# Loading and normalising the residual in one block, four transfers instead of one

## What is computed

```
m = mean(x, axis=-1);  v = var(x, axis=-1)
xn = (x - m) / sqrt(v + 1e-5)                  # the layer norm, no gain, no shift
q  = xn @ Wq.T + bq                            # 16 heads of 16
k, v = ctx @ Wk.T + bk, ctx @ Wv.T + bv        # from the context, not from x
x  = x + softmax((q k + relative terms) / 4) (v + relative terms) @ Wo.T + bo
... mixture 0, attention 1, mixture 1
```

## Time and profile before

| | us |
|---|---|
| median of three runs | 2146.1 |
| the profiled execution | 2133.87 |
| its span, first to last instruction | 2132.1 |
| TensorE busy in the span | 1902.6 |
| mean granted TensorE clock | 0.943 of full |

### The profile page before, as it was taken

The page is one execution under the profiler, slowest core; times in us unless marked ns, Lnnn a source line. Parts: engine busy times, 40 slices in busy tenths (PEclk is TensorE's granted clock), DMA queues, the critical chain, the costliest instruction groups (busy, mean ns, idle before and its releaser), DMA issues. The chain is left out here.

```text
span 2132.1 us, 40119 instructions
## 1 busy us (share of the span) xinstructions
PE 1902.6 (89%) x13656; PEld 1647.9 (77%) x13657; DVE 1329.4 (62%) x2964; ACT 1018.8 (48%) x1747; POOL 620.4 (29%) x555
## 2 busy tenths in 40 slices
PE   4788956999669999999999999999999983999994
PEld 3477956999558887887888888888888763899994
DVE  5174054667667777887787778877787875122223
ACT  2544413555246555555555565545555641444441
POOL 2300002333244423442344324422443101122220
PEclk9899967999779999999999999999999995899997
DMA  5502163111242123212322133113311218211114
GB/s 201 178 24 87 64 240 102 48 47 49 77 117 53 38 51 72 53 43 47 70 53 46 44 71 69 43 32 71 71 41 31 63 47 295 75 35 36 37 34 131
DMA packets 93663, 159.24 MB, mean 75 GB/s; under 512 B 22385, under 2 KB 54831, under 8 KB 91707
## 3 DMA queue, kind: packets, MB, share of 16 engines
q1 hardware_dynamic: 82875, 134.32, 22.4%
q0 software_dynamic: 8320, 20.65, 3.3%
q10 hardware_dynamic: 2304, 2.10, 0.3%
HBM read 71.57 MB, written 32.41 MB: 49 GB/s over the span
## 5 line engine op out<-in xcount | busy, mean ns | idle before, releaser
L1833 ACT ACTIVATE a_prob<-a_slot,a_npeak 128x848 f32<-128x848 f32 x256 | 248.4, 970 | 204.4 <-DVE a_npeak L1894 204.1
L1699 PE MATMUL a_slot<-a_KHL,a_QHL 128*128 128x424 f32 (+1 forms) x1536 | 299.5, 344 | 12.8 <-DVE a_probT L1915 10.9
L1892 DVE TENSOR_REDUCE a_part_peak<-a_slot 128x2 f32<-128x848 f32 x256 | 265.4, 1037 | 39.2 <-PE a_slot L1699 38.9
L1724 PE MATMUL a_po<-a_probT,a_V 128*64 128x256 f32 (+1 forms) x2304 | 276.8, 385 | 0.0
L1846 ACT ACTIVATE a_probT<-a_slot 128x640 f32<-128x640 f32 x256 | 180.6, 706 | 200.1 <-PE a_slot L1708 151.3
L1708 PE MATMUL a_slot<-ident,a_prob 128*128 128x128 f32 x2048 | 268.6, 275 | 0.0
L1699 PEld LDWEIGHTS a_slot<-a_KHL,a_QHL 128*128 128x128 f32 x1536 | 237.0, 190 | 39.2 <-issue 14.2
L1924 DVE CUSTOM_DVE_ANT_0 a_masked<-a_prob,a_maskr,a_latent_sum 128x253 f32<-128x253 f32 x256 | 183.5, 717 | 101.8 <-ACT a_prob L1835 86.9
L1708 PEld LDWEIGHTS a_slot<-ident,a_prob 128*128 128x128 f32 x2048 | 236.0, 142 | 8.7 <-issue 0.3
L1724 PEld LDWEIGHTS a_po<-a_probT,a_V 128*64 128x64 f32 (+1 forms) x2304 | 153.8, 136 | 83.2 <-issue 7.2
L1649 PEld LDWEIGHTS a_side<-a_W,a_latT 128*128 128x128 f32 x1536 | 193.8, 196 | 23.8 <-issue 10.8
(11 more groups left out here) (321 smaller groups left out, 3031.8 us busy)
## 6 DMA issues: line engine op xcount, KB each, us to landing
a_KHL<-a_KT SPq DMA_DIRECT2D x128, 256.0 KB, 4.4
a_QHL<-a_QT SPq DMA_DIRECT2D x128, 128.0 KB, 2.4
m_up<-_L_ffn_gate_up_proj_dram SPq DMA_DIRECT2D x8, 1024.0 KB, 9.4
m_up<-in_L_ffn_W_dram SPq DMA_DIRECT2D x8, 1024.0 KB, 9.1
m_down<-in_L_ffn_W_dram SPq DMA_DIRECT2D x8, 1024.0 KB, 12.5
a_prob_dram<-a0p_zeros SPq DMA_DIRECT2D x4, 1632.0 KB, 11.0
a_dist_dram<-a_dist SPq DMA_DIRECT2D x4, 1632.0 KB, 8.2
a_band_prob<-a_prob_dram SPq DMA_DIRECT2D x4, 1632.0 KB, 6.9
```

The source lines that it names most:

```text
L1699: ins = t_.matmul(out[:, i * BANK:i * BANK + hi - lo], q, KHL[:, pair.parity, h, part, lo:hi], start=part == 0, stop=part == 1)
L1724: ins = t_.matmul(po_t[h * D1:(h + 1) * D1, :], V[0:rows, pair.parity, j, h, :], probT[0:rows, gi % 2, j, h, :], start=j == PARTS[0][0], s ...
L1833: a_.activation(prob[:, u % 2, 0:2 * CUT].rearrange("p (n k) -> p n k", n=2), two_banks(slot[u % 2]), ACT.Exp, bias=bias, accum_out=latent ...
L1892: v.tensor_reduce(part[:, 0:2], two_banks(slot[u % 2]), AX.X, ALU.max).then_inc(part_peaked, 1)
```

## The change

`load_residual` and the weights' block are gone. `residual_norm` replaces `layer_norm`: one block in which SP issues four transfers of `x`, one for each group of four tiles and each with its own semaphore, then the identity, and then (through `load_rest`) the same twelve transfers of weights and constants in the same order. DVE waits for the transfer of group g ahead of that group's statistics, and PE waits for the identity ahead of its first transpose. The arithmetic, the sizes and the order on DVE, POOL, PE and ACT are as they were. The options of `layer_norm` that no call used are gone too.

```
+        @block.sync
+        def _(sp):
+            tiles = x.rearrange("b (t p) e -> p (b t) e", p=P)
+            for g in range(TILES // LN_GROUP):
+                cols = slice(g * LN_GROUP, (g + 1) * LN_GROUP)
+                sp.dma_start(xres[:, cols, :], tiles[:, cols, :]).then_inc(x_loaded[g], 16)
+            sp.dma_start(ident[:, :], ident_in).then_inc(ident_loaded, 16)
+            load_rest(sp)
+
         @block.vector
         def _(dve):
             def moments_of(g):
...
+                dve.wait_ge(x_loaded[g], 16)
                 for t in tiles:
-                    nc.vector.bn_stats(stats[:, t, :], src[:, t, :]).then_inc(stats_done, 1)
+                    nc.vector.bn_stats(stats[:, t, :], xres[:, t, :]).then_inc(stats_done, 1)
...
         @block.tensor
         def _(pe):
-            for t in range(TILES if dstT is not None else 0):
+            pe.wait_ge(ident_loaded, 16)
+            for t in range(TILES):
                 pe.wait_ge(dst_done, t + 1)
...
-def load_residual(nc, x, ident_in, xres, ident):
...
-            sp.dma_start(xres[:, :, :], x.rearrange("b (t p) e -> p (b t) e", p=P)).then_inc(x_loaded, 16)
-            sp.dma_start(ident[:, :], ident_in).then_inc(x_loaded, 16)
-            sp.wait_ge(x_loaded, 32)
...
-            with nc.Block() as block:
-                @block.sync
-                def _(sp):
-                    for n, dst in (("Wk", W["Wk"]), ("Wv", W["Wv"]), ("Wq", W["Wq"]), ("Wo", Wo)):
...
-            layer_norm(nc, "a0ln", xres, xn, ident, xnT)
+            def load_rest(sp):
+                for n, dst in (("Wk", W["Wk"]), ("Wv", W["Wv"]), ("Wq", W["Wq"]), ("Wo", Wo)):
...
+            residual_norm(nc, I["x"], I["ident"], xres, ident, xn, xnT, load_rest)
...
-        load_residual(nc, I["x"], I["ident"], xres, ident)
```

More of the change, by code:

```diff
@@ L83, in after, with residual_norm @@
         self.engine.wait_ge(self.sem, self.n)
-def layer_norm(nc, name, src, dst, ident, dstT=None, gain=None, shift=None, store=None):
+def residual_norm(nc, x, ident_in, xres, ident, xn, xnT, load_rest):
+    name = "a0ln"
     with phase(nc) as ctx:
@@ L98, in layer_norm @@
         turned = [ctx.enter_context(nc.psum_tensor(f"{name}_turned{i}", [P, EC, P], F32)) for i in range(4)]
+        x_loaded, ident_loaded = [sem(f"x_loaded{g}") for g in range(TILES // LN_GROUP)], sem("ident_loaded")
         stats_done, moments_done, variance_done = sem("stats_done"), sem("moments_done"), sem("variance_done")
@@ L123, in _ @@
                 for t in range(g * LN_GROUP, (g + 1) * LN_GROUP):
-                    nc.vector.tensor_scalar(dst[:, t, :], src[:, t, :], moments[:, t, 0:1], rstd[:, t:t + 1],
+                    nc.vector.tensor_scalar(xn[:, t, :], xres[:, t, :], moments[:, t, 0:1], rstd[:, t:t + 1],
                                             ALU.subtract, ALU.mult).then_inc(dst_done, 1)
@@ L142, in _ @@
                 for c in range(EC):
-                    ins = nc.tensor.transpose(turned[t % 4][:, c, :], dst[:, t, c * P:(c + 1) * P], ident[:, :])
+                    ins = nc.tensor.transpose(turned[t % 4][:, c, :], xn[:, t, c * P:(c + 1) * P], ident[:, :])
                 ins.then_inc(turned_done, 1)
@@ L147, in _ @@
         def _(act):
-            for t in range(TILES if dstT is not None else 0):
+            for t in range(TILES):
                 act.wait_ge(turned_done, t + 1)
[L150 to L157, removed]
-        @block.sync
-        def _(sp):
[L161 to L165, removed]
-def load_residual(nc, x, ident_in, xres, ident):
[L170 to L175, removed]
-            sp.dma_start(xres[:, :, :], x.rearrange("b (t p) e -> p (b t) e", p=P)).then_inc(x_loaded, 16)
-            sp.dma_start(ident[:, :], ident_in).then_inc(x_loaded, 16)
-            sp.wait_ge(x_loaded, 32)
+                nc.scalar.activation(xnT[:, :, t * P:(t + 1) * P], turned[t % 4][:, :, :], ACT.Copy).then_inc(copied, 1)
 class Context:
@@ L308, in layer0_attention @@
             loaded = sem2("loaded")
-            with nc.Block() as block:
-                @block.sync
-                def _(sp):
-                    for n, dst in (("Wk", W["Wk"]), ("Wv", W["Wv"]), ("Wq", W["Wq"]), ("Wo", Wo)):
[L313 to L321, removed]
-            layer_norm(nc, "a0ln", xres, xn, ident, xnT)
+            def load_rest(sp):
+                for n, dst in (("Wk", W["Wk"]), ("Wv", W["Wv"]), ("Wq", W["Wq"]), ("Wo", Wo)):
+                    sp.dma_start(dst[:, :, :], I["L0_xattn_" + n + "T"].rearrange("(c p) n -> p c n", p=P)).then_inc(loaded, 16)
+                sp.dma_start(ctxT[:, :, :], I["ctxT"].rearrange("(c p) n -> p c n", p=P)).then_inc(loaded, 16)
+                sp.dma_start(bq[:, :], I["L0_xattn_bq"]).then_inc(loaded, 16)
+                sp.dma_start(bk[:, :], I["L0_xattn_bk"]).then_inc(loaded, 16)
+                sp.dma_start(bv[:, :], I["L0_xattn_bv"].to_broadcast([CTX, E])).then_inc(loaded, 16)
+                sp.dma_start(rv0[:, :], I["rv_far"].to_broadcast([CTX, E])).then_inc(loaded, 16)
+                sp.dma_start(bo[:, :], I["L0_xattn_bo"].to_broadcast([P, E])).then_inc(loaded, 16)
+                sp.dma_start(mask[:, :], I["head_mask"]).then_inc(loaded, 16)
+                sp.dma_start(relk[:, :, :], I["rel_k"]).then_inc(loaded, 16)
+            residual_norm(nc, I["x"], I["ident"], xres, ident, xn, xnT, load_rest)
             pq = [c2.enter_context(nc.psum_tensor(f"a0_pq{i}", [P, BANK], F32)) for i in range(4)]
```

## The result

| | before | changed |
|---|---|---|
| first comparison, median (6 executions each) | 2135.77 us | 2119.19 us |
| ratio, 95% interval | | 0.9916, 0.9891 to 0.9941 |
| second comparison (26 and 5) | 2132.38 us | 2117.11 us, 0.9937 (0.9916 to 0.9958) |
| third comparison (16 and 9) | 2132.69 us | 2120.96 us, 0.9941 (0.9922 to 0.9959) |
| span of the profiled execution | 2132.1 us | 2117.2 us |

Forecast: 11.4 us faster, 2134.7 us. Measured: 11.7 to 16.6 us faster by the medians of three comparisons, 2119 us. The absolute number was 15.5 us off, most of it not the change's: the 2146.1 us of before was the median of three executions, and 78 further executions in the later comparisons have a median of 2133.0 us. Against that the changed kernel's 20 executions (median 2119.2 us) are 13.8 us faster, 2.4 us more than the shift.

A forecast was written before the change was run, and what follows sets the result against it. TensorE bounds the whole span, but the start is a chain of blocks separated by barriers. Norm start 16.07 to 4.7 gives -11.4 us, stalls, identity, weights and clearing 0: 2146.1 - 11.4 = 2134.7 us, range 2119 to 2146.

The forecast's parts named there:

- the shift: Whole kernel: everything behind the norm comes earlier by the norm's earlier start, 11.4 us, and the total falls by that.
- Bound and chain: Start of the kernel: 9 us of transfer, 6 us of issuing and 14 us of norm need not be in a row.
- the boundary behind the norm: End of the norm's block: the 1.10 us boundary stays, with 0 to +0.3 us for more semaphores to clear, taken as 0.
- Arrival of the first group: First block: group 0 of x is usable at 4.65, DVE starts at 4.7 instead of 16.07; bounds 4.0 and 9.3.
- No stalls, the identity hidden, the weights in time: Norm and next block: cost 0 each; later groups arrive with margins from 0.45 us, identity at 9.3, weights by 17.0.
- The splitting by itself costs nothing: First block: three further issues of x cost SP about 0.5 us each and lie under the transfer.
- rival A: First block: pieces of x land together or pay in a row; saving 6.8 or 7.7 us, time 2138 to 2141; 10%.
- The passing on through SP's clearing: Block 4: it ends with SP's clearing transfers, a chain tied to the block's start, so it moves by the full 11.4 us.
- Behind it nothing knows of absolute time but TensorE's clock: Everything behind block 4: stages keep their lengths, each 11.4 us earlier.
- The base: Whole kernel: the saving is taken off the median of 2146.1 us, not the profiled 2133.87 us, 12 us under it.
- Rival B: Behind the start: late clock returns, up to 2.1 us each, give the shift back; with twelve late +13.8 us, 2159.9 us; 5%.

The follow-up runs named there:

- four_apart: The kernel before with x in four transfers, all waited for in the first block: ratio to before 1.0008.
- zeros_early: The changed kernel with the memset of zeros and the four clearing transfers moved into the first block, behind the weights: ratio to before 0.9926.
- context_early: zeros_early with the nine small context loads also issued in the first block, ahead of the clearing: 2110.9 us, ratio to before 0.9898.
- late_inside: The changed kernel with SP first loading x whole and waiting for it inside the same block: ratio to before 0.9970.
- again1: The changed kernel run once more, unaltered: 2117.11 us, ratio to before 0.9937.
- again2: The changed kernel run a third time, unaltered: 2120.96 us, ratio to before 0.9941.
- filler_dve8: The changed kernel with eight already fulfilled waits added to DVE's program in the first block: 2124.1 us, ratio to before 0.9948.
- filler_dve: The changed kernel with four already fulfilled waits added to DVE's program ahead of its first statistics: 2119.6 us, ratio to before 0.9946.
- one_transfer: The changed kernel with x in one transfer, so DVE waits for all of it: ratio to before 0.9961.
- filler_pool: The changed kernel with eight already fulfilled waits added to POOL's program in the first block: ratio to before 0.9935.
- weights_apart: The changed kernel with the twelve weight transfers in a block of their own behind the norm: ratio to before 0.9951.
- extra_block: The changed kernel with a small block put ahead that loads only the identity and waits: ratio to before 0.9956.
- late_start: The changed kernel with the old first block ahead, x and the identity loaded, waited for, then loaded again: ratio to before 1.0000.
- filler_dve12: The changed kernel with twelve already fulfilled waits added to DVE's program in the first block: 2124.0 us, ratio to before 0.9946.

## Why the prediction was right and wrong

- **Bound and chain: right.** Three things in a row that need not be; the products moved by 11.46 us for a forecast of 11.4. That the two agree so closely is in part luck: DVE started 11.06 us earlier, and the boundary behind the norm, put at no change or up to 0.3 us more, took less (PE waits 1.22 us there instead of 1.56), which gives 0.34 us back. No run shows why it is shorter.
- **Arrival of the first group: right, 0.3 us small.** 5.01 for 4.7, within the bounds 4.0 to 9.3: from 2.5 to 3.0 us only 43 GB/s flowed with four transfers, against 223 with one.
- **No stalls, the identity hidden, the weights in time: right.** First transpose 9.77 (9.3), transfers through at 15 (17 at the latest), 5 us ahead of their use. SP's last weight issue ended at 10.64 (10.5).
- **The splitting by itself costs nothing: nearly.** 0.45 us in four_apart, where pieces that pay in a row had 7.1 us due, an estimate (rival A's 16.35 us less the 9.26 us of before); that part of rival A is out.
- **The passing on through SP's clearing: right.** zeros_early and context_early take that chain off, and the products move from 43.30 to 41.34 and 41.03 us.
- **The step that failed** is the sentence "Behind it nothing knows of absolute time but TensorE's clock", and with it the saving as a pure shift. The change also took instructions off DVE's program, a term that the sum didn't have: with 5592 instead of 5598 records three collisions with POOL's operations go the other way, 0.95 us each, 2.9 us. Time itself had no part in that: late_inside starts 7.5 us later and has the short passes. 11.4 + 2.9 = 14.3 us is inside the intervals of all three comparisons (one less the ratio, times the median of before: 12.6 to 23.3, 9.0 to 17.9 and 8.7 to 16.6 us), where 11.4 lies outside the first and inside the other two. So the 2.9 us are shown in the profiles, and the totals don't exclude a surplus of nothing or of more.
- **The base was mis-sized.** I took the saving off 2146.1, with the profiled 2133.87 in hand, and said only that they differ by 12 us. 13 us of the 15.5 us error are this median of three.
- **Rival B** (the clock gives it back) named the right source of scatter, with the wrong consequence: it moves single executions both ways (again1's and again2's profiles are 9.8 us apart, at a mean granted clock of 0.944 and 0.934), and no comparison shifted to slower. The clock's drop and return are in the records: in before PE idles from 50.34 to 54.76 us and the granted clock is 0.50 from 52.29 to 59.11; in the changed kernel PE idles from 37.09 to 43.30 and the clock is 0.50 from 39.17 to 49.41.

## What to carry to other kernels

A wait for a whole transfer, a block that only issues and a norm are three stages until they share a block; here the gain could be read off the start of the first consumer (11.06 us, and 11.46 us at the products), and it holds if the chain that ends the next block is tied to that block's start. When that chain is taken off as well, another engine ends the block: in context_early it was PE, and the slow pace of its first matmuls (2.39 us for eight, 1.29 us in the changed kernel), covered until then, came onto the path. When a stage has moved, compare the rest of the two profiles instruction by instruction before calling a surplus scatter: here the order of two engines, 0.03 us one way and 0.11 us the other, flipped with eight waits (filler_dve8) 1300 us ahead of it. And take a base time from more than three executions when the change is as small as their spread.

## What was not expected of the hardware

- The same DVE operation (line 1924 of before, 1905 of the changed kernel) took 1.52 us where POOL's `a_QT` operation (line 1613) had begun 0.03 us ahead of it, in before, and 0.48 us where it had begun 0.11 us ahead of POOL's, in the changed kernel; POOL's took 1.27 and 1.51 us.
- Eight waits on DVE that are already fulfilled (filler_dve8, four records more in its profile) and the changed kernel differ in which of the two leads 1300 us later: POOL by 0.03 us with them, DVE by 0.11 us without, and with four waits (filler_dve) POOL by 0.47 us. It is the same three passes in every profile. Whether and where DVE pauses in that pass (0.13 us, 0.32 us one operation earlier, or not at all) goes with them. The operation takes 0.48 us at 5592 records (after, again1, again2, one_transfer, late_inside, filler_pool, zeros_early, context_early), 1.14 at 5594 (filler_dve, weights_apart), 1.52 at 5596 and 5598 (extra_block, late_start, filler_dve8; before, four_apart, filler_dve12). The pass as a whole takes 15.7 us in the first group and 16.6 in both others.
- The first eight matmuls behind the norm took 1.29 us or 2.39 to 2.42 us, and the clock records of the sixteen traces sort them without exception. The nine with 1.29 have a record of full clock as the last one ahead of these matmuls (18.69 against 20.07 us in the changed kernel). Of the seven others, five have no record until later (35.22 against 31.51 us in before, 23.51 against 20.30 in again1), and late_start and weights_apart had fallen back to 0.50. The rows print 1.00 for the time without a record, but the matmuls of those five took 2.39 us, as in late_start (2.39 us) and weights_apart (2.42 us), whose last record is 0.50. The same program falls on either side: again1 took 2.39 us, again2 1.29.
